# A graph-attention and expert kernel: the visit table padded to whole turns of four groups, and the experts' first bias moved from VectorE to a one-row matmul

## The reference, cut to what matters

```
def gat_layer(x, W, al, ar, bias, src, dst, H, D, use_elu):      # H, D = 12, 64 / 12, 64 / 1, 768
    z = (x @ W).reshape(N, H, D)
    e = leaky_relu((z*al).sum(-1)[src] + (z*ar).sum(-1)[dst], 0.2)
    ex = exp(e - segment_max(e, dst)[dst])
    alpha = ex / segment_sum(ex, dst)[dst]
    out = segment_sum(alpha[:, :, None] * z[src], dst) + z + bias
    return elu(out) if use_elu else out

x = x + gat_layers(layernorm(x))
t = layernorm(x);  vals, idx = top_k(t @ Wr.T, 2);  r = softmax(vals)
h = gelu(t @ Wi[e].T + bi[e])                 # 192 columns for each expert e
x = x + sum over the two experts of r * (h @ Wo[e].T + bo[e])
```

## Time and profile before

| | |
|---|---|
| time, median of 3 runs | 3006.99 us (3005.36 to 3008.19) |
| the profiled execution, its own time | 3008.19 us, of which the span of the profile is 3006.5 us |
| TensorE (PE) busy | 2652.1 us, 88% of the span |
| VectorE (DVE) busy | 2078.4 us, 69% |
| GpSimd (POOL) busy | 1486.1 us, 49% |
| ScalarE (ACT) busy | 1244.2 us, 41% |
| granted TensorE clock, mean | 0.936 of 2.4 GHz |

### The profile page before, as it was taken

One profiled execution on the slowest core, in us unless ns is written; L12 is line 12 of the kernel. 1 busy time (PEld: TensorE's weight loads), 2 busy tenths in 40 slices (PEclk: granted clock), 3 DMA queues, 4 the chain that ended last, 5 costly groups with the idle time before them and its releaser, 6 DMA issues.

```text
span 3006.5 us, 57078 instructions
## 1 busy us (share of the span) xinstructions
PE 2652.1 (88%) x14127; PEld 1896.9 (63%) x14131; DVE 2078.4 (69%) x3890; ACT 1244.2 (41%) x2582; POOL 1486.1 (49%) x1478
## 2 busy tenths in 40 slices
PE   3997999999979889999997998999999875698886
PEld 2885666656568756666665885666665575676664
DVE  6776999999877589999997774656655596322221
ACT  1224656666534356666664442333333342011111
POOL 1005777777500177777771005777777410033433
PEclk9998999999989999999998998999999955599998
DMA  4337999999744399999994458999999798056665
GB/s 164 110 112 254 350 339 348 343 345 343 248 143 159 131 355 348 346 350 341 343 344 158 157 177 284 347 333 339 346 339 335 281 401 278 26 106 125 118 125 90
DMA packets 204551, 765.15 MB, mean 255 GB/s; under 512 B 33574, under 2 KB 65462, under 8 KB 204232
## 3 DMA queue, kind: packets, MB, share of 16 engines
q0 software_dynamic: 120432, 584.47, 57.0%
q1 hardware_dynamic: 66280, 130.94, 13.8%
q10 hardware_dynamic: 17760, 48.79, 4.2%
HBM read 662.67 MB, written 101.79 MB: 254 GB/s over the span
## 4 chain that ended last, share of the span: by engine, by line
PE 43%; DMA 17%; DVE 15%; issue 12%; POOL 8%; ACT 4%; ACTq 1%; DVEq 1%; POOLq 0%; SPq 0%
PE PS L892 31%; POOL arena L546 6%; DMA out<-arena,target_of 6%; PE PS L821 5%; DMA arena<-table,src_k 4%; DMA W<-table,src_k 3%; PE PS L823 2%; POOL W L546 2%; PE PS L867 2%; DVE arena L1154 2%; DVE arena L1170 2%; DVE arena L1169 2%; DVE arena L1179 1%; ACT arena L608 1%; DMA arena<-mixed 1%
## 5 line engine op out<-in xcount | busy, mean ns | idle before, releaser
L546 POOL DMA_INDIRECT arena<-table,src_k x945 | 966.5, 1023 | 296.7 <-issue 241.3
L892 PE MATMUL PS<-arena,S 128*128 128x384 f32 (+1 forms) x1848 | 679.8, 502 | 17.8 <-DVE arena L1295 9.1
L1295 DVE TENSOR_TENSOR arena<-arena,PS 128x768 f32<-128x768 f32 x630 | 576.0, 948 | 0.9 <-ACT arena L687 0.9
L892 PEld LDWEIGHTS PS<-arena,S 128*128 128x128 f32 x1848 | 338.6, 191 | 205.4 <-issue 45.5
L821 PE MATMUL PS<-W_split,S 128*128 128x512 f32 x900 | 352.8, 410 | 19.7 <-DVE xT_rest L1195 19.5
L892 PE MATMUL PS<-parts,S 128*128 128x384 f32 (+2 forms) x1332 | 330.2, 370 | 44.5 <-DVE parts L1312 23.4
L546 POOL DMA_INDIRECT W<-table,src_k x300 | 313.7, 1046 | 91.4 <-issue 64.6
L512 POOL DMA_DIRECT2D table<-arena x75 | 40.9, 546 | 636.2 <-DVEq L1191 427.9
L892 PE MATMUL PS<-arena,S_weighted 128*128 128x384 f32 (+1 forms) x840 | 304.5, 501 | 12.7 <-DVE S L1297 10.0
L867 PEld LDWEIGHTS PS<-erp,ST_b 128*128 128x128 bf16 x3735 | 172.6, 96 | 195.4 <-issue 130.8
L892 PEld LDWEIGHTS PS<-parts,S 128*128 128x128 f32 x1332 | 221.3, 190 | 86.5 <-issue 77.6
(11 more groups left out here) (258 smaller groups left out, 4222.9 us busy)
## 6 DMA issues: line engine op xcount, KB each, us to landing
local_b<-local SPq DMA_DIRECT2D x249, 160.0 KB, 5.8
mixed<-sums ACTq DMA_DIRECT2D x75, 384.0 KB
arena<-mixed SPq DMA_DIRECT2D x75, 384.0 KB, 3.7
arena<-table SPq DMA_DIRECT2D x75, 384.0 KB, 5.3
table<-arena POOLq DMA_DIRECT2D x50, 396.0 KB, 2.8
arena<-in_x SPq DMA_DIRECT2D x48, 384.0 KB, 7.3
arena<-table,src_k POOLq DMA_INDIRECT x945, 6.1
table<-arena POOLq DMA_DIRECT2D x25, 384.5 KB, 4.9
```

The source lines that it names most:

```text
L546: nc.gpsimd.indirect_dma_start(edge_row(l, k % U)[:, 0:table_width(l)], None, table[l][:, :], bass.IndirectOffsetOnAxis(src_k[:, k:k + 1]. ...
L892: o = nc.tensor.matmul(flat[:, bass.ds(odd * 1024 + 512 * c, n)], onehot, row[:, c * HALF:c * HALF + n], start=False, stop=True, skip_grou ...
L1295: nc.vector.tensor_tensor(z, z, a, ALU.mult).then_inc(s_msg, 1)
```

## The change

It has two parts.

1. V is rounded up to a multiple of 20 in place of a multiple of 5: from 415 to 420. Each of the three edge sweeps then has 84 groups in place of 83, and its last turn has four groups like all others. The five added visits of a sweep have one-hot matrices of zeros only (their destinations are set to `NO_NODE`, -1, which is one more instruction on VectorE, once), and all engines do their full work on them: five gathers of real table rows, one load of `local_b`, the one-hots, the weights, the multiplications and the matmuls. VectorE's program has one written-out copy of the loop body less, and its loop one turn more.
2. In the experts, VectorE's `add_bias` is gone. TensorE adds the bias by a seventh matmul of `up`, whose stationary operand is one row of ones and whose moving operand is the expert's 192 values of bi on one partition; ScalarE's Gelu reads PSUM directly. bi is loaded to one partition (6 KB) and not to 128 (768 KB). `up` of slot n waits for the Gelu of slot n - 2, where before it waited for the bias of slot n - 1.

```diff
 U = G * NBUF
-VISITS = ET + NB - 1
-V = -(-VISITS // G) * G
+V = -(-(ET + NB - 1) // U) * U
 NG = V // G
-NI = -(-NG // NBUF)
-LAST_GROUPS = NG - (NI - 1) * NBUF
+NI = NG // NBUF
...
-        bi_rows = W_rest[:, 0:F]
+        bi_row = W_rest[0:1, 0:F]
...
-            sp.dma_start(bi_rows, ffn["bi"].rearrange("e f -> (e f)").partition_broadcast(P)).then_inc(s_bi, 16)
+            sp.dma_start(bi_row, ffn["bi"].rearrange("e f -> (e f)").rearrange("(o n) -> o n", o=1)).then_inc(s_cload, 16)
...
             def gelu(b):
-                act.wait_ge(s_biased, b.n + 1)
-                nc.scalar.activation(h_rows(b.q), h_rows(b.q), ACT.Gelu).then_inc(s_gelu, 1)
+                act.wait_ge(s_up, b.n + 1)
+                if b.reuse:
+                    act.wait_ge(s_hTp, b.n - 1)
+                nc.scalar.activation(h_rows(b.q), PS[:, 2, b.q * 256:b.q * 256 + FF], ACT.Gelu).then_inc(s_gelu, 1)
...
-                    groups = LAST_GROUPS if last else NBUF
-                    for jj in range(groups):
+                    for jj in range(NBUF):
...
-            pe.wait_ge(s_cload, 16 * 3)
+            pe.wait_ge(s_cload, 16 * 4)
...
-                if b.n:
-                    pe.wait_ge(s_biased, b.n)
+                if b.reuse:
+                    pe.wait_ge(s_gelu, b.n - 1)
                 for k in range(KC):
-                    o = nc.tensor.matmul(to, xT(b.q)[:, k * P:(k + 1) * P], WiT[:, k, bass.ds(e * FF, FF)],
-                                         start=(k == 0), stop=(k == KC - 1))
-                o.then_inc(s_up, 1)
+                    nc.tensor.matmul(to, xT(b.q)[:, k * P:(k + 1) * P], WiT[:, k, bass.ds(e * FF, FF)],
+                                     start=(k == 0), stop=False)
+                nc.tensor.matmul(to, ones[0:1, :], bi_row[:, bass.ds(e * FF, FF)], start=False, stop=True).then_inc(s_up, 1)
...
-                if V > VISITS:
-                    link(nc.vector.memset(dst_k[:, VISITS:V], NO_NODE))
-                dve.sem_inc(s_tables, 1)
+                nc.vector.memset(dst_k[:, VISITS:V], NO_NODE).then_inc(s_tables, 1)
...
-                body(0)
-                with dve.Fori(1, NI - 2) as i:
+                body(0, False)
+                with dve.Fori(1, NI - 1) as i:
                     dc.enter(i - 1, (1 if H > 1 else 3) * NBUF)
-                    body(i)
-                dc.leave(NI - 3)
-                body(NI - 2, NBUF + LAST_GROUPS)
-                body(NI - 1, LAST_GROUPS)
+                    body(i, False)
+                dc.leave(NI - 2)
+                body(NI - 1, True)
...
-            def add_bias(b):
-                if b.q == 0:
-                    owners[:] = nc.values_load_multi_w_load_instructions(
...
-                dve.wait_ge(s_up, b.n + 1)
-                if b.reuse:
-                    dve.wait_ge(s_hTp, b.n - 1)
-                nc.vector.tensor_tensor(h_rows(b.q), PS[:, 2, b.q * 256:b.q * 256 + FF], bi_rows[:, bass.ds(owners[b.q] * FF, FF)],
-                                        ALU.add).then_inc(s_biased, 1)
-
-            dve.wait_ge(s_bi, 16)
-            sweep_nodes(dve, [(add_bias, 0), (copy_y, -1), (copy_hT, 0)], count=NS)
+            sweep_nodes(dve, [(copy_y, -1), (copy_hT, 0)], count=NS)
```

More of the change, by code:

```diff
@@ L38 @@
 SPLIT = ((2, 7, 10, 12, 17), (2, 7, 10, 12, 17), (1, 4, 7, 11, 14, 17))
+VISITS = ET + NB - 1
 RING = 6
@@ L296, in split_before @@
         def split_before(l):
[L297 to L302, removed]
+            return NI * sum(len(x) for x in SPLIT[:l])
         def prep(at, n):
@@ L702, in body @@
                 def body(i, last, first=False):
-                    groups = LAST_GROUPS if last else NBUF
-                    for jj in range(groups):
+                    for jj in range(NBUF):
                         g = NBUF * i + jj
                         leading(g, i, jj)
-                        if not (last and jj == groups - 1):
+                        if not (last and jj == NBUF - 1):
                             weights(g + 1, (jj + 1) % NBUF)
@@ L710, in body @@
                             close_blocks(g - 1)
-                        if H > 1 and (not last or jj + 2 < groups):
+                        if H > 1 and not (last and jj >= NBUF - 2):
                             one_hots(g + 2, (jj + 2) % NBUF)
@@ L896, in body @@
                 def body(i, last):
-                    groups = LAST_GROUPS if last else NBUF
-                    for jj in range(groups):
+                    for jj in range(NBUF):
                         g = NBUF * i + jj
-                        ahead = not last or jj + ER_LEAD < groups
+                        ahead = not (last and jj >= NBUF - ER_LEAD)
                         now = blocks_of(g)
@@ L1245, in turned @@
                 def turned(g, i, jj):
-                    dve.wait_ge(s_lb[jj], 16 * i + 16 * (uses(jj) * l + 1))
+                    dve.wait_ge(s_lb[jj], 16 * i + 16 * (NI * l + 1))
                     nc.vector.tensor_scalar(ST_b[:, jj, :], local_b[:, jj, :], own[:, 0:1], None,
@@ L1258, in logits @@
                         for j in range(jj * G, (jj + 1) * G):
-                            dve.wait_ge(s_z[j], 16 * i + 16 * (uses(jj) * l + 1))
+                            dve.wait_ge(s_z[j], 16 * i + 16 * (NI * l + 1))
                         dc.mark(nc.vector.tensor_tensor(u, edge_heads(l, jj), er[:, :, 0:H], ALU.add))
@@ L1333, in weigh, with body @@
                             steps[3]()
-                def body(i, left=NG):
-                    for jj in range(min(NBUF, left)):
+                def body(i, last):
+                    for jj in range(NBUF):
                         g = NBUF * i + jj
-                        more = jj + 1 < left
+                        more = not (last and jj == NBUF - 1)
                         steps = exponents(g + 1, i + (jj + 1) // NBUF, (jj + 1) % NBUF) if more else None
-                        weigh(g, i, jj, steps, left > NBUF + jj)
+                        weigh(g, i, jj, steps, not last)
                 if H == 1:
@@ L1528, in copy_hT @@
                 nc.vector.tensor_copy(hT(b.q)[0:FH, :], PS[0:FH, 3, 2 * b.q * P:(2 * b.q + 2) * P]).then_inc(s_hT, 1)
-            owners = [None, None]
-            def add_bias(b):
-                if b.q == 0:
-                    owners[:] = nc.values_load_multi_w_load_instructions(
-                        expert_at[0:1, bass.ds(b.turn, 1), 1:3].rearrange("o s j -> o (s j)"),
-                        engines=[mybir.EngineType.DVE], min_val=0, max_val=EX - 1,
-                        skip_runtime_bounds_check_because="a sum of EX comparisons, limited to EX - 1")[1]
-                dve.wait_ge(s_up, b.n + 1)
-                if b.reuse:
-                    dve.wait_ge(s_hTp, b.n - 1)
-                nc.vector.tensor_tensor(h_rows(b.q), PS[:, 2, b.q * 256:b.q * 256 + FF], bi_rows[:, bass.ds(owners[b.q] * FF, FF)],
-                                        ALU.add).then_inc(s_biased, 1)
-            dve.wait_ge(s_bi, 16)
-            sweep_nodes(dve, [(add_bias, 0), (copy_y, -1), (copy_hT, 0)], count=NS)
+            sweep_nodes(dve, [(copy_y, -1), (copy_hT, 0)], count=NS)
 _INS = ["x", "edges"] + [f"L0_gnn_{n}{i}" for i in range(3) for n in ("W", "al", "ar", "b")] + [
```

1 line of the change is left out of this document (removed).

## The result

The changed kernel takes 3025.41 us (median of 4 runs, 3021.3 to 3029.1), the kernel before in the same measurement 3006.18 us (3001.77 to 3008.19): +19.2 us, ratio 1.0065 with a 95% interval of 1.0048 to 1.0083. It is slower, and 3026.0 had been forecast (+19.0). In a second measurement the change took 3019.79 us against 3002.45, ratio 1.0059 (1.0044 to 1.0074).

The account below looks back on a forecast made before the run. TensorE's visits were taken to bound the edge sweeps and the chain of adds the experts. The terms 19.8 + 0.1 + 1.1 + 0 - 2.0 = +19.0 us on 3006.99 gave 3026.0 us, range 3019 to 3031.

Parts of the forecast that it names:

- One more group in each sweep: Edge sweeps: the added group is not hidden and costs 6.6 us a sweep, +19.8 us for three.
- The bias matmul: Experts' `up`: 0.35 us more per TensorE step, hidden under the adds; only the first slots pay, +1.1 us.
- VectorE's bias add: Experts: removing the add and changing the waits makes no engine wait longer, 0 us (-0.5 to +0.3).
- The smaller load: Layer norm: 762 KB less of bi in flight relieves the late `normed` store, -2.0 us (-4.5 to 0).
- no relief: Layer norm: Wo's packets take bi's place, so the smaller load gains nothing; +21.0 us, 3028; chance 0.25.
- second rival: Layer norm: Wo fills bi's turns on the DMA engines, no gain from the smaller load; 3028 us, chance 0.25.
- the third: Rival at the layer norm: both stalls vanish with the smaller load; +6.8 us, 3014; chance 0.08.
- the fourth: Rival in the experts: TensorE becomes the bound through the one-row matmul, loop 19 us longer; 3045; chance 0.04.
- the sixth: Rival in the edge sweeps: the added group is hidden and costs next to nothing; 3006 us, chance 0.04.

Follow-up runs that it names:

- e1: Kernel before with only the change's second part (one-row bias matmul, narrow bi load): 3008.68 us against 3002.45, ratio 1.0020.
- e5: The kernel of e1 run again: 3006.29 us against 3002.66 for the kernel before, ratio 1.0014.
- e6: The kernel of e1 with four further one-row matmuls ahead of each `up`, results overwritten: 3083.37 us (+81).
- e7: The kernel of e1 with two further one-row matmuls ahead of each `up`, results overwritten: 3042.97 us (+40).
- e8: Kernel before with bi, bo and Wo loaded only after the layer norm: 2994.91 us, ratio 0.9975.
- e0: The changed kernel measured and profiled again: 3019.79 us against 3002.45 for the kernel before.
- e2: Kernel before with only the change's first part (84 groups a sweep in place of 83): 3016.39 us, ratio 1.0046.
- e3: The changed kernel with V = 440, four more empty groups a sweep (88): 3099.33 us, ratio 1.0334 to the kernel before.
- e9: The kernel of e1, but bias by a 128-row matmul (identity stationary, bi on 128 partitions): 3232.05 us against 3230.85, ratio 1.0005.
- e10: The kernel of e8 with the last block's 53-row load of x split into 48 and 5 rows: 3218.21 us against 3230.85 before, ratio 0.9969.
- e12: The kernel before, unchanged, run once more on the third chip for a second profile: 3233.61 us.
- e11: The changed kernel with bi loaded to 128 partitions as before: 3252.79 us against 3230.85 for the kernel before, ratio 1.0072.

## Why the prediction was right

**One more group in each sweep: right, size right.** Forecast 6.6 us a sweep. The profiles near 3000 us with 83 groups (before, e1, e5, e6, e7, e8) have 18 sweeps with a mean of 553.0 us (546.9 to 558.8), those with 84 (the change, e0, e2) nine with 560.8 (554.7 to 563.8), e3 three of 88 with 585.2. That is 7.8 us for the first added group and 6.4 for each of five. On the third chip (e9, e10 and e12 against e11) it is 638.0 - 630.7 = 7.3. By time, e3's +96.9 less the second part's 2 to 6 us is 6.1 to 6.3 for each of 15 groups, and e2's +13.9 less than that. The values lie on both sides of the forecast, and +19.8 agrees with all but e2, by which the three groups are 8 to 19 us. Nothing hides a group, because all that follows waits for its last visit, as the earlier trace rows had it. One reading was off: the first sweep's visits begin at 263.32 us and not at 270.05, where the chain of waits enters them, so that sweep has 6.73 us a group and not 6.65, which changes nothing in the sum.

**The bias matmul: covered as forecast, but mis-sized.** The prediction took it as a full matmul, 0.35 us, and a step of 5.77. It is 0.67 and 6.09: the term had left out the idle time before the weight load at each change between 128 rows and one. The conclusion held, since 6.09 is still under the 6.5 of the adds, but the reserve is 0.4 us and not 0.75, and e7, forecast with the wrong size, came out at +40 in place of +3. On the first slots the forecast was +1.1 us. With the one-row matmul (the change, e0, e1, e5) the time from the routing to the first add is 96.6, 97.0, 96.8 and 96.3 us; without it (before, e2, e8) 95.9, 95.2 and 95.5: +1.1. Two more profiles with the one-row matmul, e3 and e11, are left out of this mean: they have 101.9 and 99.9 us, since TensorE's clock rose later there (last section). Over all six the term would be 2.5 us, and whether the change has a part in the later rise is not shown.

**VectorE's bias add: nothing, as forecast.** The adds took 358.5, 356.0 and 359.6 us with it (before, e2, e8) and 354.4, 358.7, 354.3 and 358.5 without it (the change, e0, e1, e5), means of 358.0 and 356.5, a difference within their scatter.

**The smaller load: the step that failed.** Forecast -2.0 us, and the rival "no relief" had 0.25. The two stalls together are 14.2, 11.6, 13.9, 13.0 and 10.4 us with the wide load (before, e2, e9, e12, e11), mean 12.6, and 15.0, 13.6, 12.8, 14.3, 15.1, 14.7 and 14.7 with the narrow one (the change, e0, e1, e5, e6, e7, e3), mean 14.3: about 1.7 us more with the narrow load, with a scatter of 1 to 2 us in each group. The whole stage, from the end of the sweeps to the routing, is 2.2 us longer with it (means of 148.9 and 146.7).

The clearest part is VectorE's wait, which is 9.8 to 10.8 us in all five profiles with the wide load and 11.3 to 12.3 in all seven with the narrow one; three of the five are from the third chip and none of the seven is. The prediction had left this wait where it was, because its load is issued before bi, and had taken it for a wait for `mixed`; e10 shows that it is the 53 rows of x, which are in flight for 18 to 22 us, by the last two landing signals, and so beside all that is issued behind them. The packets in the traces show what takes bi's place: the first packet of Wo (48 KB each) starts 5.8 to 7.3 us after the issue of `mixed` in all five profiles with the wide load, and 4.3 to 4.9 us after it in all seven with the narrow one. So Wo comes forward by 1 to 3 us. That this is what delays x is consistent with e8, where the bulk loads were moved away and the wait fell to 6.66 us, but was not tested by itself. The prediction's second rival had this right: by the rule that the DMA engines take turns between the queues that have work (the Trainium skill, DMA: Bandwidth & Descriptors, Queues, rings and completion order) it expected no gain, and there was none. The bytes of a load were the wrong measure: what counts is what takes its place.

**The sum.** With the corrected terms it is 19.8 + 0.1 + 1.1 + 1.7 = +22.7 us; measured are +19.2, +17.3 and, with the wide load on the third chip, +21.9. So the corrected sum is less close than the forecast was. By the times of the parts the sum splits in another way: the first part alone took +13.9 us where 19.9 was forecast, and the second +6.2 and +3.6 where -0.9 was, together 17.5 to 20.1. The agreement of 19.0 with 19.2 is luck in part: one term was too high or at the edge of its interval, another had the wrong sign, and the two stood against each other. And the chances that the prediction puts outside its range (half of the third, the fourth, the sixth) add up to 0.13, not 0.17.

**What stays open.** The second part alone measured +6.2 and +3.6 us with intervals that begin at +2 and +1, and its stages account for 1.1 + 1.7 = 2.8. Whether the rest is scatter, the later rise of the clock in some executions, or something in the sweeps, whose code it doesn't touch, these runs can't tell. Nor do they tell why three groups alone came to 13.9 us by time and to 23 by the mean of the sweeps. Part of it is which executions were profiled: with 83 groups they lie 3.4 us below the medians of their kernels on average, with 84 groups 1.3 us above.

## What to carry to other kernels

Rounding a loop up to whole turns is not free where the loop's last iteration releases the next stage: the padding costs its full price, once for each pass (three groups, 14 to 23 us here by the several measurements), and that price can be read from the pieces of the chain before the change is built. A matmul with one contraction row for a bias costs more than one with all rows when it stands between full ones (0.67 against 0.32 us), so with bi on 128 partitions anyway the identity does it cheaper. And when a wait is put down to a transfer, look at all the transfers that it waits for, and at how many rows each has: the stalls at the layer norm belonged in part to bulk loads that nobody needs for another 100 us, and in part to a load of 53 rows, and without both the kernel before is 12.6 us faster.

## What the runs showed of the hardware

A weight load of one row behind one of 128, and one of 128 rows behind one of one, was not brought forward under the running matmul: there are 0.23 us of idle time before each of the two in every step, and none with 128 rows in that place (e9). It is not every change of the row number: the 96-row load of `down` behind the 128-row transposes has no idle time before it. The Trainium skill (TensorE: Matmul & The Clock Gate, Part 2) says that loads are pulled ahead of matmuls in flight when their row groups do not conflict or when they go to the background weight buffer; the change between 128 rows and one is a case in which these runs saw no pulling ahead.

A load of 53 rows, 159 KB, held up the last block by about 6 us (6.66 in e8, 0.72 in e10, with the bulk loads out of the way in both); as 48 rows and 5 rows it did not. This agrees with the Trainium skill (DMA: Bandwidth & Descriptors, Why a DMA increments its semaphore by 16 and not by 1), which says that the number of engines is the largest up to 16 that divides the row count, one for 53.

Edge sweeps of 83 groups took 553 us on two chips and 631 us on a third. The other stages of the kernel before differ little between its first profile and that on the third chip, e12 (from the end of the sweeps to the routing 148.9 and 145.9 us, from there to the first add 95.9 and 96.0, the adds 358.5 and 358.7). The first line is a stretch of an edge sweep of before on the third chip (e12), the second is the first profile of the changed kernel; columns as in the earlier trace rows:

```profile
1500.00:1600.00 100.00, 94.26 (x477) 56.89 (x476) 83.45 (x123) 55.52 (x132) 65.93 (x67) 1.00 0.92 304
```

```profile
1500.00:1600.00 100.00, 97.64 (x527) 61.93 (x526) 93.44 (x139) 63.48 (x152) 76.71 (x76) 0.98 0.96 344
```

The DMA engines move 304 GB/s and not 332 to 344 and are as busy as before, and TensorE and VectorE do less in the same time: 477 matmuls in 100 us where the earlier trace rows has 522. From 1100 to 1600 us VectorE's first instruction of each group (L1278), which waits for the gathers and for TensorE's lookups, finds the engine idle for 80 us in e12 and for 30 in before. That the gathers set the pace of the sweeps there is the likely reading; most of these waits in e12 the profile doesn't name.

In the experts' first slots TensorE runs at 1.2 GHz (granted clock 0.50) for most or all of slot 0's `up`, after short waits and, before them, some 40 us of unbroken work in the routing, also at 0.50. In the change the second slot's `up` ran at 2.4 GHz and took 2.21 us, as it did in e0, e1, e5 and all profiles without the one-row matmul; in e11 and e3, with the same code, it was still at 1.2 GHz, with 4.20 us. The first line is the change's second `up`, the second that of e11:

```profile
2639.98:2642.19 2.21, 2.21 (x13) 1.99 (x13) 0.00 (x0) 0.00 (x0) 0.00 (x0) 1.00 0.00 0
```

```profile
2875.15:2879.35 4.20, 4.20 (x13) 3.76 (x13) 0.00 (x0) 0.00 (x0) 0.00 (x0) 0.50 0.00 0
```

This is 2 us of the 3 to 5 by which the first add came later in these two (99.9 and 101.9 us after the routing). In e6 and e7, which have more one-row matmuls, slot 1's `up` was also slower, 4.21 and 3.60 us.
